# Scores of two cross-attentions: half of the key columns in four 64x64 quadrants of the array instead of two 64x128 row halves

## The reference

```python
x = x + L0_xattn(layernorm(x), ctx_1024, Wq, Wk, Wv, Wo, bo)       # 8 heads of 64
x = x + L0_attn(layernorm(x), ...)                                  # delta rule, 4 heads
x = x + L0_ffn(layernorm(x), ...)                                   # 15 experts, top 3
x = x + L1_xattn(layernorm(x), ctx_1024, ctx_1024, bias, Wq, ...)   # 16 heads of 64
x = x + L1_attn(layernorm(x), ...)                                  # quantised attention
x = x + L1_ffn(layernorm(x), ...)                                   # recurrent cell
```

## Time and profile before

| | |
|---|---|
| median of 3 runs | 1941.63 us (1941.47 to 1942.94) |
| profiled execution, its own time | 1944.34 us |
| its span, from first to last instruction | 1942.5 us |
| TensorE busy | 1853.7 us |
| VectorE busy | 1569.4 us |
| mean granted TensorE clock | 0.976 of full |
| plain stage | from about 31 to 535 us |
| biased stage | from about 821 to 1839 us |

### The profile page before, as it was taken

One profiled execution on the slowest core, in us unless ns is written; L12 is line 12 of the kernel. 1 busy time (PEld: TensorE's weight loads), 2 busy tenths in 40 slices (PEclk: granted clock), 3 DMA queues, 4 the chain that ended last, 5 costly groups with the idle time before them and its releaser, 6 DMA issues. The chain is left out here.

```text
span 1942.5 us, 44495 instructions
## 1 busy us (share of the span) xinstructions
PE 1853.7 (95%) x17440; PEld 1271.3 (65%) x17451; DVE 1569.4 (81%) x2178; ACT 857.8 (44%) x1173; POOL 924.3 (48%) x438
## 2 busy tenths in 40 slices
PE   7999999999877989999999999999999999999788
PEld 4667666666646868867666666667666766666545
DVE  4666766677777746699999999999999999999884
ACT  3666666676531135433444344434433344434401
POOL 0346655575560034206655565547555665557300
PEclk9999999999989879999999999999999999999889
DMA  3000110000030032100000000020000000000000
GB/s 138 10 15 0 59 56 14 0 14 9 7 142 1 2 150 87 38 9 2 14 14 14 0 14 14 25 85 5 14 14 14 0 14 14 14 0 9 12 40 11
DMA packets 27773, 52.80 MB, mean 27 GB/s; under 512 B 4259, under 2 KB 15284, under 8 KB 27188
## 3 DMA queue, kind: packets, MB, share of 16 engines
q1 hardware_dynamic: 27232, 51.57, 8.0%
q10 hardware_dynamic: 468, 0.16, 0.0%
HBM read 51.20 MB, written 0.52 MB: 27 GB/s over the span
## 5 line engine op out<-in xcount | busy, mean ns | idle before, releaser
L358 POOL TENSOR_TENSOR biased_sums<-biased_sums,biased_scores 128x1024 f32<-128x1024 f32 x216 | 512.6, 2373 | 138.5 <-ACT biased_scores L663 118.8
L729 DVE TENSOR_TENSOR biased_scores<-ps,bias 128x1024 f32<-128x1024 f32 x256 | 311.6, 1217 | 35.2 <-PE ps L446 33.9
L743 DVE TENSOR_TENSOR ps<-ps,biased_scores 128x512 f32<-128x512 f32 x480 | 332.9, 693 | 4.1
L750 DVE TENSOR_TENSOR biased_scores<-biased_scores,ps 128x1024 f32<-128x1024 f32 x256 | 305.7, 1213 | 3.4 <-PE ps L504 2.7
L663 ACT ACTIVATE biased_scores<-biased_scores 128x1024 f32<-128x1024 f32 x256 | 263.0, 1052 | 97.3 <-DVE biased_scores L750 95.3
L358 POOL TENSOR_TENSOR plain_sums<-plain_sums,plain_scores 128x1024 f32<-128x1024 f32 x104 | 246.6, 2371 | 60.5 <-ACT plain_scores L663 50.1
L743 DVE TENSOR_TENSOR ps<-ps,plain_scores 128x512 f32<-128x512 f32 x240 | 167.3, 697 | 118.1 <-ACT plain_scores L646 113.3
L446 PE MATMUL ps<-biased_queries,keys_again 64*128 64x256 f32 x2048 | 257.3, 390 | 3.6 <-DVE biased_scores L729 2.8
L458 PE MATMUL ps<-biased_scores,biased_values 128*64 128x256 f32 x2048 | 245.2, 382 | 3.6 <-ACT biased_scores L663 3.2
L393 PE MATMUL ps<-weights_again,context_again 128*64 128x128 f32 x4096 | 248.0, 274 | 0.0
L393 PEld LDWEIGHTS ps<-weights_again,context_again 128*64 128x64 f32 x4096 | 228.5, 137 | 28.8 <-issue 17.9
(11 more groups left out here) (409 smaller groups left out, 2274.7 us busy)
## 6 DMA issues: line engine op xcount, KB each, us to landing
moe_w<-in_moe_w SPq DMA_DIRECT2D x32, 256.0 KB, 2.7
weights_again<-in_wqkv SPq DMA_DIRECT2D x45, 128.0 KB, 2.2
context<-in_ctx_t SPq DMA_DIRECT2D x4, 1024.0 KB, 6.7
context_again<-in_ctx_t SPq DMA_DIRECT2D x4, 1024.0 KB, 7.4
bias<-in_fside SPq DMA_DIRECT2D x1, 4096.0 KB, 15.3
biased_w_out<-in_w_out SPq DMA_DIRECT2D x16, 256.0 KB, 2.6
context<-in_ctx_t SPq DMA_DIRECT2D x2, 1536.0 KB, 9.6
context_again<-in_ctx_t SPq DMA_DIRECT2D x2, 1536.0 KB, 9.6
```

The lines of the kernel that those rows point to most:

```text
L358: pool.tensor_tensor(both(SUM[:, :, :, :]), both((E[:, 0] if kp == 1 else SUM)[:, :, :, :]), both(E[:, kp, :, :, :]), ALU.add).then_inc(su ...
L729: dve.tensor_tensor(E[:, kp, :, :, :].rearrange("p (h t) n j -> p h t (n j)", h=2), scores_bank(kp).rearrange("p (h t n) -> p h t n", h=2, ...
L743: ins = dve.tensor_tensor(to, highest, E[:, kp, :, n, :], ALU.max)
L750: dve.tensor_tensor(at, at, c.ps[:, LOWER, :].rearrange("p (a j) -> p a j", a=HQ).unsqueeze(2) .to_broadcast([P, HQ, 2, P]), ALU.add).then ...
```

## The change

In `scores`, the products of the second 128 keys of each `kp` (n = 1) are issued as two, for 64 keys each. The stationary operand is then 64 rows x 64 columns, and the result goes to 64 partitions: with the two heads these are four tiles of 64x64, one for each quadrant of the array. The products of the first 128 keys (n = 0) stay at 64x128. Nothing else changes; results go to the same places in PSUM, and the semaphores are the same. Lines behind this one move by two.

```diff
-                            last = pe.matmul(out, KT[half, at:at + P], QS[half, :].rearrange("p (t j) -> p t j", t=2),
-                                             start=True, stop=True)
+                            for keys_of in HALVES if n else (slice(0, P),):
+                                last = pe.matmul(out[keys_of, :, :], KT[half, at + keys_of.start:at + keys_of.stop],
+                                                 QS[half, :].rearrange("p (t j) -> p t j", t=2),
+                                                 start=True, stop=True)
```

## The result

The changed kernel takes a median of 2037.7 us (2035.74 to 2039.16, 4 runs) against 1941.87 us of before in the same session: 1.0483 times as long, with a 95% interval of 1.047 to 1.0496. The forecast was 2038 us.

A forecast was written before the change was run, and what follows sets the result against it. The prediction took TensorE to bound both stages. Three new shape changes, 0.50 us a block over 192 blocks, add 96 us to 1941.6, with nothing given back: some 2038 us, range 1999 to 2065.

The forecast's parts named there:

- What bounds the kernel: Both cross-attention stages run at TensorE's pace; VectorE has 3.6 us of slack in a biased sweep.
- No streaming cost: In scores, four quadrants run side by side, so each kp's n = 1 part still takes 2 x 0.217 us.
- A one-sided change of shape costs as much as a two-sided one: In scores, steps between 64x128 and 64x64 cost a 0.10 us drain plus open load, 0.05 or 0.10 us.
- rival 2: In scores, part of the shape-change price is missing: 2009 us, or 2000 if loads hide; chance 0.08.
- The sum for a block: Three new shape changes in a scores block cost 0.50 us together; 192 blocks make 96 us.
- What is given back: TensorE's waits for VectorE in biased sweeps could return 3 us; taken as nothing.
- The rule weighed: Skill's rule that TensorE matmuls keep strict program order, blocking the next tile's; by an earlier trace row, the forecast sum holds instead.
- the third rival: In scores, quadrants run two at a time, 167 us more on top of 96: 2205 us; chance 0.10.
- the free step: In scores, the step between row mode and quadrants costs nothing: 1941.6 us; chance 0.05.
- the missing part of the price: In scores, the step from quadrants to column mode is free, 2009 us, or loads hide, 2000; chance 0.08.
- two at a time: In scores, each kp's n = 1 part takes 4 x 0.217 us instead of 2 x 0.217: 2205 us; chance 0.10.
- faster: In scores, both new kinds of step and the block's last step are free, 29 us less: 1913 us; chance 0.03.

The follow-up runs named there:

- e1: All scores products in 64x64 tiles, none in 64x128, plus an empty instruction per scores call, against the kernel before: ratio 0.9968.
- e2: The changed kernel's products, n = 1 first in odd kp (rows, quadrants, quadrants, rows), plus an empty instruction: 1.0332 of before.
- e3: The changed kernel's products, n = 1 first in even kp (quadrants, rows, rows, quadrants), plus an empty instruction: 1.0298 of before.
- e4: Against the kernel before, only the second 128 keys of the odd kp in quadrants (rows, rows, rows, quadrants): ratio 1.0154.
- e6: The kernel before in row mode, with both n of head 0 ahead of both of head 1 in each kp: ratio 1.009.
- e8: The kernel before in row mode, with each kp's four products in the order head 0, 1, 1, 0: ratio 1.0005.
- e7: Against the kernel before, scores made in column mode over both heads at once, changing what is computed, with as many streamed columns: ratio 0.9791.

## Why the prediction was right, point by point

- What bounds the kernel: right. Both stages ran at TensorE's pace, and a sweep grew by what was added to its list. In the plain stage a sweep grew by 4.18 us, which is the growth of its blocks, 8 x 0.52, within rounding. In the biased stage it grew by 3.95, from 63.03 to 66.98.
- No streaming cost: right. e1 shows four tiles side by side at the same 0.22 us for each step; the case that had only a hint in the earlier trace rows is now measured.
- A one-sided change of shape costs as much as a two-sided one: right. This was the weakest step, argued from 128x128 to 128x64 because the trace lacked the step itself. It was weaker than the prediction says: the run behind that step also waited for ScalarE's copy of the queries, which on ScalarE's timeline of before ends at 198.07 + 0.38 = 198.45 us, the very moment from which the 0.09 us counts:

```profile
198.07 0.38 ACT L640 ACTIVATE plain_queries<-ps 128x256 f32<-128x256 f32 x1 [0.27 <-PE ps L421]
```

So the 0.09 us that is empty in the earlier trace rows could as well have been that wait, and the row could not tell. The experiments can: e2, e3 and e4 price the step at 0.15 to 0.16 us into the quadrants and about 0.21 out of them. And the last step of a block, from quadrants to column mode, costs what the step from rows did: had it been free, as rival 2 had it, the block would be 0.15 shorter than the 2.45 measured.
- The sum for a block: 0.50 forecast, 0.52 measured. The missing 0.02 is the stagger, which I named and took as nothing: the third and fourth tile of a quadrant run start a few ns behind each other, and a drain counts from the last, about 0.01 for each of the two runs. 192 x 0.52 is 100 us instead of 96.
- What is given back: wrong, but small. I took it as nothing, with a bound of 3 us, because the last kp's maxima would stay late by a fixed chain. They did not: the waits for VectorE shrank, at the scores from 11.1 to 2.6 us and at the maxima from 13.7 to 10.1 us. Before, a biased sweep was 63.03 - 62.80 = 0.23 us longer than a plain one; in the changed kernel both take 66.98. Over 15 sweeps that is 3.5 us, and 100 us of blocks became 95.8 us between the medians. The two small errors, 4 us of stagger and some 4 us given back, cancel; that the forecast met the median within 0.3 us is partly luck, the size of the term is not.
- The rule weighed: program order of matmuls, as the Trainium skill has it (TensorE: Matmul & The Clock Gate, on packing small matmuls), does not hold across tiles here. By it e6 would be 1.11 times before at the least, by the estimate above, and is 1.009; the third rival, which the prediction ties to it, gave 2205 us for the changed kernel, which took 2037.7.
- The rivals: the free step, the missing part of the price, two at a time, and faster are each excluded by a block length above. The faster one had a true core: with the same tile throughout, quadrants do win 0.04 us a block, but only where no row run stands between them.

## What to carry to other kernels

Count changes of TensorE's tile shape as you count waits: here each costs 0.10 us plus the first weight load in the open, 0.05 for 64 and 0.10 for 128 columns, and it shows in no view as a wait for another engine, only as idle "issue" time of the weight loads and as a first record longer than the rest. Smaller tiles that cover the same array neither gained nor lost here by themselves (float32, 256 moving columns, 0.22 us a step in both shapes), so choose one shape for as long a run as the waits allow, and put products of unlike shape at its ends. The trace of before priced a step that it never contained, through two neighbours that each changed one side alone; look whether such a neighbour also stands behind a wait, as the earlier trace rows did, before relying on it.

## What the runs showed of the hardware that was not expected

- The order of products for tiles matters a little although tiles overtake each other: with four records of one tile ahead of the other's, right behind a wait, the other tile's first weights came 0.10 us late (e6), while the same four records inside a kp cost nothing (e8).
- Four 64x64 tiles start in one after the other within about 0.02 us and then keep that offset; the only place where it was seen to cost is ahead of a change of shape.
- Taking all shape changes around the scores away (e7, which computes something else with as many streamed columns) is worth 2.8 us of a plain sweep of 62.8: the kernel before spends 4.5% of the plain stage's sweeps on them.
